# Two-block steps in the last stage, epsilon added by VectorE, and an earlier schedule of gathers and sums in the second attention

## The chip, the cores and the metric

The kernel runs on one core of one Trainium2 chip. The metric is the device time of one execution in microseconds. Engines are called PE (TensorE), DVE (VectorE), ACT (ScalarE), POOL (GpSimd) and SP (SyncE, which only issues DMAs here).

## The reference, cut to what matters

```python
x = x + tanh(g_xattn[0]) * attention_0(layernorm(x), ctx, ctx)        # 8 key groups of 8
x = x + tanh(g_ffn[0])   * experts(layernorm(x), ...)                 # 64 experts, the best 8 of each token, and a shared one
x = x + tanh(g_xattn[1]) * (attention_1(layernorm(x), ctx, ctx) @ Wc.T + bc)   # 4 key groups of 16
x = x + tanh(g_ffn[1])   * fp8_mlp(layernorm(x), w_fc, w_proj)
# fp8_mlp: both matrices and both inputs are scaled by their largest magnitude and rounded to fp8;
# h = square(relu(x8 @ w8_fc.T * scales)), rounded to fp8 again, then h8 @ w8_proj.T * scales
```

x is 64 x 64 tokens of 256 numbers, so 4096 rows: 32 tiles of 128 rows, or 8 chunks of 512.

## The kernel before, in words

x stays in SBUF. There are five stages: the first attention; the router, which scatters the rows to the experts; the experts, whose results go to DRAM (`ys`); the second attention, from about 803 to 1085 us; and the fp8 MLP. The order on each engine is written out by hand, and semaphores join the engines.

**The second attention** is a software pipeline of steps t = -3 to 35 (`second_step`, L1137). In step t an engine works on tile t and its neighbours: the normalised query of tile t+3 (`query`), the statistics of tile t+4 (`stats`, L993), the result of tile t-3 added to x (L1153), its statistics for the MLP, and the normalised tile t-4 (L1165). Into these steps the end of the experts' stage is woven for the tiles of the second half (18 tiles of 8 rows per token, 144 gathers and 144 sums):

- POOL gathers the experts' rows by indirect DMA (`gather`, L737; the instruction is L744). `asked(t)` (L733) says how many are issued before step t. Gather n first waits until gather n-5 has landed (L741), and the first of a tile waits until the tile's buffer, one of three, has been summed out.
- DVE adds each gathered row, times its weight, to x (`combine`, L1438; the instruction is L1453). `sums_within` (L1462) spreads the sums over six places of each step. The first sum of a tile waits until all 8 of its gathers have landed.
- The normalisation needs 1/sqrt(variance + epsilon). In `deviations` (L653) POOL waits for DVE's mean and variance (`mv`), adds epsilon (L663), waits for that and takes the power -0.5 (L665). In POOL's step this stands behind two of the step's gathers and ahead of the others (L720 to L729). DVE waits for the result (`rs2`, L1159) ahead of the norm and the query, for which the deviations of the step before count. The call for step t needs the statistics that DVE makes at the end of step t.

SP loads the MLP's weights and the values (V, in three parts) of the second attention while the first steps run. After some steps DVE also works on those weights: `weight_scales` (two maxima over 128x2048, L1013, after steps -1 and 0, small pieces after steps 2 and 3) and `weight_rounding` (three operations on 128x1024 after each of steps 5 to 8).

**The MLP** has a first pass (`first_pass`), which finds the largest hidden value, and a second one, the last stage of the kernel. There each of 8 chunks of 512 rows has 8 blocks f of 128 hidden features (`NF`), and each block is 128x512. For a block PE makes the product in a PSUM bank (L1879), four banks in turn. ACT takes relu with a scale (L984) into R and squares it (L978) into HS, and does the relu of the next block ahead of the square of this one. DVE rounds to a grid in three operations: CC (L1566, a bf16 result from f32), UU (L1568, bf16 from bf16 and f32) and H8 (L1572, all bf16). R, HS, CC and UU have four buffers each, used in turn. When all blocks of a chunk are rounded, PE does the 32 matmuls of the second product (`project`, L1894), which stand on PE behind the next chunk's hidden blocks. DVE ends each chunk with two operations of the chunk before (L1582, `finish`), and SP stores them. For the last chunk PE follows block by block (L1928 on), and two rows of products come after the last block.

Of the kernel before, what the change touches and what calls it, by code (L numbers as in the profile page):

```python
# [4 lines left out]
ALU = mybir.AluOpType  # L5
# [4 lines left out]
BF16 = mybir.dt.bfloat16  # L10
# [44 lines left out]
FGRP = 4  # L55
LAST = (NT + 1, NT + 3)
# [111 lines left out]
def inside(t):  # L168

    return not known(t) or 0 <= t < NT  # L170
# [37 lines left out]
def flamingo_block(nc, x_in, ctx, ctxT, gates, consts, wpairs, wsmall, wshdown, wc_in, bc_in, wfc_in, wproj_in, out):  # L208
# [128 lines left out]
    R, HS = ([carve([CH]) for _ in range(4)] for _ in range(2))  # L337
    CC, UU = ([carve([CH], BF16) for _ in range(4)] for _ in range(2))
# [134 lines left out]
    with nc.Block() as block:  # L473
# [23 lines left out]

        @block.sync
# [140 lines left out]
        def _(pool):  # L639
# [13 lines left out]
            def deviations(t, j):  # L653

                n = t + 5
                if inside(t + 4):
                    pool.wait_ge(LNA["mv"], STAT_BASE[2] + t + 5)
                if inside(t - 3):
                    pool.wait_ge(LND["mv"], t - 2)
                a, z = (j if inside(t + 4) else 3 - j), (3 - j if inside(t - 3) else j)  # L660
                at = slice(min(a, z), max(a, z) + 1, abs(z - a) or 1)
                k = 1 + (a != z)
# [132 lines left out]
        def _(act):  # L795
# [175 lines left out]
            def squares(c, j):  # L971

                def square(f):
                    n = c * NF + f
                    act.wait_ge(F["r_ready"], n + 1)
                    if past(c, 1) or f >= 4:
                        act.wait_ge(F["hu_done"], n - 3)
                    act.activation(HS[f % 4], R[f % 4], ACT.Square).then_inc(F["hs_ready"], 1)  # L978

                for f in range(NF):  # L980
                    if past(c, 1) or f >= 4:
                        act.wait_ge(F["hs_ready"], c * NF + f - 3)
                    act.wait_ge(F["h_ready"], NCH * NF // FGRP + c * NF + f + 1)
                    act.activation(R[f % 4], bank[f % 4][:, :], ACT.Relu, scale=FS[:, 22:23]).then_inc(F["r_ready"], 1)  # L984
                    if f:
                        square(f - 1)
                square(NF - 1)
# [4 lines left out]
        def _(dve):  # L992
# [62 lines left out]
            def attention(layer, a):  # L1055
# [83 lines left out]
                def second_step(t, q):  # L1139
# [34 lines left out]
                    if inside(t + 4):  # L1174
                        if t + 4 >= HT:
                            dve.wait_ge(M["cb"], ADDS * (t + 5))
                        stats(t + 4, j, ln)

                if layer == 0:
                    sweep(dve, first_step, LAST[layer], 12)  # L1180
                else:
                    stats(0, 0, ln)
                    for t in range(-3, LAST[layer] + 1):
# [378 lines left out]
            def rounding(c, j):  # L1562
                for f in range(NF):
# [4 lines left out]
                    dve.tensor_tensor(UU[f % 4], CC[f % 4], HS[f % 4], ALU.subtract).then_inc(F["hu_done"], 1)  # L1568
# [3 lines left out]
                    dve.tensor_tensor(H8[j][:, f, :], CC[f % 4], UU[f % 4], ALU.subtract).then_inc(F["h8_ready"], 1)  # L1572
# [17 lines left out]
        def _(pe):  # L1590
# [306 lines left out]
            def project(c, j):  # L1897
                pe.wait_ge(F["h8_ready"], (c + 1) * NF)
# [8 lines left out]
            def second_pass(c, j):  # L1907
                for f in range(NF):
# [5 lines left out]
                    if past(c, 1) or f >= 4:  # L1914
                        pe.wait_ge(F["r_ready"], c * NF + f - 3)
# [11 lines left out]
            for f in range(NF):  # L1927
                pe.wait_ge(F["h8_ready"], c * NF + f + 1)  # L1928
                for i in (0, 2):
                    product(j, i, f)  # L1930
# [48 lines left out]
```

## Time and profile before

| | us |
|---|---|
| median of 3 runs | 1263.76 (1261.61 to 1265.2) |
| the profiled execution | 1256.04 |
| its span | 1254.2 |
| DVE busy | 1049.4 (84%) |
| PE busy | 888.8 (71%) |
| POOL busy | 726.9 (58%) |
| ACT busy | 703.2 (56%) |
| mean granted clock of TensorE | 0.872 |

Times of the trace are microseconds from the start of the span. Shares of the whole span say little, as the stages have different limits. "Idle before" in a row is the time that the engine stood still ahead of the instruction, and the arrow names what ended it.

### The profile page before, as it was taken

The numbers are of one execution on the slowest core, as the hardware profiler recorded it, in microseconds if no ns is written. First come the engines' busy times: TensorE is split into PE (matmuls) and PEld (weight loads), VectorE is DVE, ScalarE is ACT, GpSimd is POOL, SyncE is SP. The second block draws the span as 40 slices with busy tenths as digits, with TensorE's granted clock in tenths as the row PEclk, the third lists the DMA queues.
The fourth block names the chain that finished last, engine by engine and source line by source line (L and its number), as shares of the span: only waits on it lengthen the run. The fifth ranks groups of instructions, "written<-read, shape, count | busy, mean of one in ns | idle before, by whom it ended". The sixth has DMA issues, their size and how long they took to land. (4 is left out here: it accounts for less than half of the span.)

```text
span 1254.2 us, 31305 instructions
## 1 busy us (share of the span) xinstructions
PE 888.8 (71%) x9384; PEld 630.4 (50%) x9394; DVE 1049.4 (84%) x2645; ACT 703.2 (56%) x1370; POOL 726.9 (58%) x800
## 2 busy tenths in 40 slices
PE   4789994455517787778687878657787678576665
PEld 2445552343306676767576776535555456322332
DVE  5789997988817899887699999858987778598998
ACT  3679994455406665665455666435454455426763
POOL 3467773777777777755356655267887872290000
PEclk9899995555559999999899999878899999799887
DMA  4987772222248999999799999683233330000111
GB/s 123 261 241 217 223 231 74 90 94 99 100 142 286 353 345 345 344 316 286 250 304 315 315 323 322 202 174 89 77 93 92 91 93 18 1 0 1 34 50 50
DMA packets 198115, 221.50 MB, mean 177 GB/s; under 512 B 44958, under 2 KB 176863, under 8 KB 197727
## 3 DMA queue, kind: packets, MB, share of 16 engines
q1 hardware_dynamic: 173406, 152.72, 39.4%
q0 software_dynamic: 24576, 67.14, 16.6%
q8 instruction: 68, 1.11, 0.4%
q14 instruction: 65, 0.52, 0.1%
HBM read 114.66 MB, written 105.12 MB: 175 GB/s over the span
## 5 line engine op out<-in xcount | busy, mean ns | idle before, releaser
L1745 PE MATMUL bank<-arena,region 128*128 128x128 f16 x2496 | 227.1, 229 | 2.2 <-DVE arena L1471 1.8
L767 POOL DMA_INDIRECT xs<-V x176 | 177.4, 1008 | 66.3 <-issue 50.1
L1819 PE MATMUL bank<-arena 128*128 128x128 f16 x1536 | 151.8, 223 | 69.3 <-DMA arena<-xs 68.7
L1745 PEld LDWEIGHTS bank<-arena,region 128*128 (+1 forms) x2496 | 173.3, 103 | 9.2 <-issue 2.8
L1819 PEld LDWEIGHTS bank<-arena 128*128 128x128 f16 x1536 | 102.1, 100 | 79.2 <-DMA arena<-xs 78.7
L929 ACT COPY arena<-bank 128x1024 f16<-128x1024 f16 x96 | 96.8, 1009 | 70.0 <-PE bank L1819 68.0
L814 ACT ACTIVATE arena<-bank 128x512 f32<-128x512 f32 x192 | 108.1, 605 | 46.0 <-PE bank L1629 45.5
L944 ACT CAST arena<-arena 64x512 f16<-64x512 f32 x96 | 59.3, 618 | 132.2 <-DVE arena L1487 132.2
L1076 DVE TENSOR_REDUCE arena<-bank 128x8 f32<-128x512 f32 x192 | 122.6, 679 | 12.1 <-PE bank L1615 10.4
L1848 PE MATMUL bank<-region,arena 128*128 x384 | 92.1, 279 | 47.2 <-DVE arena L1501 30.5
L744 POOL DMA_INDIRECT arena<-ys,idx x88 | 90.3, 1027 | 54.8 <-DVE x L1453 27.8
L744 POOL DMA_INDIRECT region<-ys,idx x96 | 96.0, 1000 | 27.1 <-issue 26.8
L1471 DVE COPY arena<-bank 128x1024 f16<-128x1024 f16 x96 | 65.5, 683 | 53.4 <-PE bank L1819 51.3
L1643 PE MATMUL bank<-arena 128*32 128x256 f32 (+1 forms) x768 | 74.8, 406 | 43.1 <-DVE arena L1088 43.1
L744 POOL DMA_INDIRECT V<-ys,idx x72 | 75.2, 1044 | 43.5 <-DVE x L1453 23.3
L1879 PE MATMUL bank<-region 128*128 (+1 forms) x246 | 69.9, 412 | 35.9 <-ACT arena L984 20.8
L767 POOL DMA_INDIRECT xs<-arena,V x80 | 80.1, 1001 | 24.4 <-issue 22.6
L1849 PE MATMUL bank<-region,arena 128*128 x384 | 91.5, 277 | 0.0
L1629 PE MATMUL bank<-arena,KDS 32*128 32x256 f32 (+1 forms) x768 | 79.5, 428 | 0.7 <-ACT arena L836 0.4
L1494 DVE COPY arena<-bank 128x512 f32<-128x512 f32 x96 | 66.4, 692 | 7.3 <-PE bank L1849 4.3
L1848 PEld LDWEIGHTS bank<-region,arena 128*128 128x128 f16 x384 | 37.8, 99 | 68.2 <-issue 63.3
L1487 DVE TENSOR_TENSOR arena<-bank,arena 64x512 f32<-64x512 f32 x96 | 66.6, 693 | 4.8 <-ACT arena L940 1.4
(232 smaller groups left out, 2269.9 us busy)
## 6 DMA issues: line engine op xcount, KB each, us to landing
arena<-xs SPq DMA_DIRECT2D x384, 128.0 KB
ys<-arena SPq DMA_DIRECT2D x96, 512.0 KB
xs<-idx SPq DMA_DIRECT2D x52, 256.0 KB, 3.1
arena<-in_wpairs SPq DMA_DIRECT2D x32, 256.0 KB, 2.9
arena<-in_wpairs SPq DMA_DIRECT2D x64, 128.0 KB, 3.2
out<-arena SPq DMA_DIRECT2D x16, 256.0 KB, 2.2
xs<-idx SPq DMA_DIRECT2D x8, 384.0 KB, 3.6
xs<-V POOLq DMA_INDIRECT x176
```

The lines of the kernel that those rows point to most:

```text
L744: pool.indirect_dma_start(SLOTS[half_of(t)][t % NSLOT][:, k * H:(k + 1) * H], None, ys[half_of(t)], bass.IndirectOffsetOnAxis(ap=idx[:, t, ...
L767: pool.indirect_dma_start(xs[half_of(t)], bass.IndirectOffsetOnAxis(ap=at_row[:, t, n % 8:n % 8 + 1], axis=0), ROW[t % NROW], None).then_i ...
L814: act.activation(EX[4 * j + n], bank[4 + n], ACT.Exp, scale=d ** -0.5).then_inc(a["ex_ready"], 1)
L929: act.copy(XTP[g % 2][:, 0:2], tpm[0]).then_inc(R_["xt"], 1)
L1076: dve.tensor_reduce(XG[q][:, gp * 2 * gpu:(gp + 1) * 2 * gpu, :].rearrange("p g (m w) -> p g m w", w=rp)[:, :, r * n:(r + 1) * n, 2 * d:2 ...
L1629: mm = pe.matmul(bank[4 + n][:, b * 256:(b + 1) * 256], KD[q][rows, b, :], Q2[q % 2][rows, :, b * S:(b + 1) * S], start=True, stop=True)
L1643: mm = pe.matmul(bank[1][n * cg:(n + 1) * cg, b * 256:(b + 1) * 256], VD[j][:, b, n * cg:(n + 1) * cg], EX[4 * j + n][:, b * 256:(b + 1) * ...
L1745: mm = pe.matmul(o, lhs(a, w, k), rhs(a, w, k), start=(n == 0), stop=(n == 3 * KT - 1))
L1819: mm = pe.transpose(tpm[q // 2][:, q % 2, m, :], RAW[g % 2][:, q, m * P:(m + 1) * P], rcv("ident"))
L1848: pe.matmul(o, IH[j][:, q, :], wx, start=True, stop=False)
L1849: mm = pe.matmul(o, IL[j][:, q, :], wx, start=False, stop=True)
L1879: mm = pe.matmul(bank[at][:, :], WF8[:, k, f * P:(f + 1) * P], X8[:, k, bass.ds(c * CH, CH)], start=(k == 0), stop=(k == KT - 1))
```

## The change

In the last stage the unit of work is a pair of blocks. R, HS, CC and UU have two buffers of 128x1024 in place of four of 128x512, and ACT and DVE issue 32 of each operation in place of 64. PE still makes blocks, but waits once per pair. In the second attention DVE adds epsilon itself, at the end of each step (`widened`), and POOL's `deviations` keeps the wait and the power. `asked` issues 4, 6 and 8 gathers in steps -3, -2 and -1, where 2, 2 and 3 stood, and then 4.97 per step where 5.48 stood. `sums_within` begins in step -1 where it began in step 1, does 4.97 sums per step where 5.33 stood, and ends in step 27 as it did.

```diff
+NFP = NF // 2
-    R, HS = ([carve([CH]) for _ in range(4)] for _ in range(2))
-    CC, UU = ([carve([CH], BF16) for _ in range(4)] for _ in range(2))
+    R, HS = ([carve([2 * CH]) for _ in range(2)] for _ in range(2))
+    CC, UU = ([carve([2 * CH], BF16) for _ in range(2)] for _ in range(2))
...
             def deviations(t, j):
-                if inside(t + 4):
-                    pool.wait_ge(LNA["mv"], STAT_BASE[2] + t + 5)
-                if inside(t - 3):
-                    pool.wait_ge(LND["mv"], t - 2)
-                pool.tensor_tensor(ve[:, at, :], mv[:, at, 1:2], epsilon[:, :].unsqueeze(1).to_broadcast([P, k, 1]), ALU.add).then_inc(ve2, 1)
-                pool.wait_ge(ve2, n)
+                at, k = columns_of(t, j)
+                pool.wait_ge(ve2, t + 5)
                 pool.tensor_tensor(rs[:, at, :], ve[:, at, :], neghalf[:, :].unsqueeze(1).to_broadcast([P, k, 1]), ALU.pow).then_inc(rs2, 1)
...
             def asked(t):
-                return max(2 * (t + 3), 0) if t < 0 else min(7 + (8 * HALF[1] - 7) * t // 25, 8 * HALF[1])
+                return (0, 4, 10)[t + 3] if t < 0 else min(9 + ADDS * HALF[1] * (t + 2) // 29, ADDS * HALF[1])
...
                 def square(f):
-                    n = c * NF + f
+                    n = c * NFP + f
                     act.wait_ge(F["r_ready"], n + 1)
-                    if past(c, 1) or f >= 4:
-                        act.wait_ge(F["hu_done"], n - 3)
-                    act.activation(HS[f % 4], R[f % 4], ACT.Square).then_inc(F["hs_ready"], 1)
+                    if past(c, 1) or f >= 2:
+                        act.wait_ge(F["hu_done"], n - 1)
+                    act.activation(HS[f % 2], R[f % 2], ACT.Square).then_inc(F["hs_ready"], 1)
...
+                for f in range(NFP):
+                    if past(c, 1) or f >= 2:
+                        act.wait_ge(F["hs_ready"], c * NFP + f - 1)
+                    act.wait_ge(F["h_ready"], NCH * NF // FGRP + c * NF + 2 * f + 2)
+                    act.activation(R[f % 2], bank8[:, f % 2 * 2 * CH:(f % 2 + 1) * 2 * CH], ACT.Relu, scale=FS[:, 22:23]).then_inc(F["r_ready"], 1)
...
+            def widened(t, j):
+                if inside(t + 4):
+                    dve.wait_ge(LNA["mv"], STAT_BASE[2] + t + 5)
+                if inside(t - 3):
+                    dve.wait_ge(LND["mv"], t - 2)
+                at, k = columns_of(t, j)
+                dve.tensor_scalar(ve[:, at, :], mv[:, at, 1:2], EPS, None, ALU.add).then_inc(ve2, 1)
...
                         stats(t + 4, j, ln)
+                    if inside(t + 4) or inside(t - 3):
+                        widened(t, j)
...
-                first, last = (min(max((SUM_PARTS * (t - 1) + part + z) * HALF[1] * ADDS // (SUM_PARTS * 27), 0), HALF[1] * ADDS) for z in range(2))
+                first, last = (min(max((SUM_PARTS * (t + 1) + part + z) * HALF[1] * ADDS // (SUM_PARTS * 29), 0), HALF[1] * ADDS) for z in range(2))
...
             def rounding(c, j):
-                for f in range(NF):
-                    n = c * NF + f
+                for f in range(NFP):
+                    n = c * NFP + f
                     dve.wait_ge(F["hs_ready"], n + 1)
-                    dve.tensor_scalar(CC[f % 4], HS[f % 4], SHORT_GRID, SHORT_FLOOR, ALU.mult, ALU.max).then_inc(F["hc_done"], 1)
+                    if past(c, 1) or f >= 2:
+                        dve.wait_ge(F["h8_ready"], n - 1)
+                    dve.tensor_scalar(CC[f % 2], HS[f % 2], SHORT_GRID, SHORT_FLOOR, ALU.mult, ALU.max).then_inc(F["hc_done"], 1)
...
-                    dve.tensor_tensor(H8[j][:, f, :], CC[f % 4], UU[f % 4], ALU.subtract).then_inc(F["h8_ready"], 1)
+                    dve.tensor_tensor(H8[j][:, 2 * f:2 * f + 2, :].rearrange("p f t -> p (f t)"), CC[f % 2], UU[f % 2], ALU.subtract).then_inc(F["h8_ready"], 1)
...
-                    if past(c, 1) or f >= 4:
-                        pe.wait_ge(F["r_ready"], c * NF + f - 3)
+                    if f % 2 == 0 and (past(c, 1) or f >= 4):
+                        pe.wait_ge(F["r_ready"], c * NFP + f // 2 - 1)
```

## Rows read from the trace of the kernel before

**Rows 1.** Windows: length; busy (count) PE, PEld, DVE, ACT, POOL; clock, DMA share, GB/s.
```profile
909.90:1032.50 122.60, 93.13 (x808) 63.95 (x806) 99.22 (x281) 61.09 (x138) 97.88 (x114) 0.94 0.33 93
...
1150.00:1200.00 50.00, 34.56 (x184) 19.12 (x188) 47.75 (x97) 35.74 (x61) 0.00 (x0) 0.90 0.10 32
```

**Rows 2.** Timeline, POOL: start, length, what [idle before]; between the last two, five gathers.
```profile
992.22 0.20 POOL L663 TENSOR_TENSOR ve<-mv,epsilon 128x2 f32<-128x2 f32 x1
992.50 0.72 POOL L665 TENSOR_TENSOR rs<-ve,neghalf 128x2 f32<-128x2 f32 x1
...
999.63 0.29 POOL L663 TENSOR_TENSOR ve<-mv,epsilon 128x2 f32<-128x2 f32 x1
```

**Rows 3.** Timeline, DVE: from one step's norm and query to the next one's.
```profile
984.64 0.73 DVE L1010 TENSOR_SCALAR arena<-x,mv,rs 128x256 f32<-128x256 f32 x2 [0.88 <-POOL rs L665]
...
990.92 0.34 DVE L1101 TENSOR_SCALAR arena<-KDS,cst 128x256 f16<-128x256 f32 x1
993.26 0.74 DVE L1010 TENSOR_SCALAR arena<-x,mv,rs 128x256 f32<-128x256 f32 x2 [2.00 <-POOL rs L665]
```

**Rows 4.** Timeline, POOL: deviations of steps 5, 9 and 24.
```profile
869.68 1.12 POOL L663 TENSOR_TENSOR ve<-mv,epsilon 128x2 f32<-128x2 f32 x1
...
909.99 0.23 POOL L663 TENSOR_TENSOR ve<-mv,epsilon 128x2 f32<-128x2 f32 x1
...
1032.47 0.25 POOL L663 TENSOR_TENSOR ve<-mv,epsilon 128x2 f32<-128x2 f32 x1
```

**Rows 5.** Timeline, first steps: weights' maximum, gathers 7 and 15, first sums of tiles.
```profile
820.22 2.29 DVE L1013 TENSOR_REDUCE FS<-region 128x1 f32<-128x2048 f32 x1 [4.26 <-DMA region<-in_wproj]
...
826.05 0.99 POOL L744 DMA_INDIRECT region<-ys,idx  x1 [0.18 <-issue]
827.03 1.28 DVE L1076 TENSOR_REDUCE arena<-bank 128x8 f32<-128x512 f32 x2
...
832.52 1.02 DVE L1453 SCALAR_TENSOR_TENSOR x<-region,x 128x256 f32<-128x256 f32 x2 [4.21 <-DMA region<-ys,idx]
...
840.09 0.96 POOL L744 DMA_INDIRECT arena<-ys,idx  x1 [0.30 <-issue]
...
843.07 1.00 DVE L1453 SCALAR_TENSOR_TENSOR x<-arena,region,x 128x256 f32<-128x256 f32 x2 [3.58 <-DMA arena<-ys,idx]
```

**Rows 6.** DMA, 818:824 and 824:830, the gathers' queue: packets, MB, share.
```profile
q0 software_dynamic: 208, 0.57, 46.3%
...
q0 software_dynamic: 102, 0.26, 22.1%
```

**Rows 7.** Timeline, last stage: two ends of chunks and one block between.
```profile
1165.00 1.40 DVE L1582 SCALAR_TENSOR_TENSOR arena<-bank,FS,x 128x512 f32<-128x512 f32 x2
1165.23 5.33 PE L1894 MATMUL bank<-region 128*128 128x256 bf16 x32 [1.69 <-DVE region L1572]
...
1169.43 0.42 DVE L1566 TENSOR_SCALAR arena<-arena 128x512 bf16<-128x512 f32 x1
...
1169.89 0.69 DVE L1568 TENSOR_TENSOR arena<-arena 128x512 bf16<-128x512 bf16 x1
...
1170.61 0.42 DVE L1572 TENSOR_TENSOR region<-arena 128x512 bf16<-128x512 bf16 x1
...
1178.57 1.40 DVE L1582 SCALAR_TENSOR_TENSOR arena<-bank,FS,x 128x512 f32<-128x512 f32 x2
```

**Rows 8.** Timeline, start of the first pass: DVE operations on 1024 columns.
```profile
1088.62 0.69 DVE L1043 TENSOR_SCALAR arena<-arena 128x1024 f32<-128x1024 f32 x1 [1.29 <-ACT arena L961]
...
1090.67 1.22 DVE L1527 TENSOR_TENSOR region<-arena 128x1024 bf16<-128x1024 f32 x1
```

**Rows 9.** Timeline: relu before the first block; an ACT operation on 1024 columns; PE's end.
```profile
1093.62 1.13 ACT L964 ACTIVATE arena<-region,FS 128x1024 f32<-128x1024 f32 x1
...
1138.74 1.27 ACT L984 ACTIVATE arena<-bank,FS 128x512 f32<-128x512 f32 x2 [28.64 <-DVE FS L1555]
...
1246.55 4.02 PE L1894 MATMUL bank<-region 128*128 128x256 bf16 x18 [0.91 <-DVE region L1572]
```

More of the change, by code:

```diff
@@ L496, in got_all, with columns_of @@
                 eng.wait_ge(got[i], got_count(i, 8 * (tile + 1)))
+        def columns_of(t, j):
+            a, z = (j if inside(t + 4) else 3 - j), (3 - j if inside(t - 3) else j)
+            return slice(min(a, z), max(a, z) + 1, abs(z - a) or 1), 1 + (a != z)
         @block.sync
@@ L653, in deviations @@
             def deviations(t, j):
-                n = t + 5
-                if inside(t + 4):
-                    pool.wait_ge(LNA["mv"], STAT_BASE[2] + t + 5)
-                if inside(t - 3):
-                    pool.wait_ge(LND["mv"], t - 2)
-                a, z = (j if inside(t + 4) else 3 - j), (3 - j if inside(t - 3) else j)
-                at = slice(min(a, z), max(a, z) + 1, abs(z - a) or 1)
-                k = 1 + (a != z)
-                pool.tensor_tensor(ve[:, at, :], mv[:, at, 1:2], epsilon[:, :].unsqueeze(1).to_broadcast([P, k, 1]), ALU.add).then_inc(ve2, 1)
-                pool.wait_ge(ve2, n)
+                at, k = columns_of(t, j)
+                pool.wait_ge(ve2, t + 5)
                 pool.tensor_tensor(rs[:, at, :], ve[:, at, :], neghalf[:, :].unsqueeze(1).to_broadcast([P, k, 1]), ALU.pow).then_inc(rs2, 1)
@@ L973, in square @@
                 def square(f):
-                    n = c * NF + f
+                    n = c * NFP + f
                     act.wait_ge(F["r_ready"], n + 1)
-                    if past(c, 1) or f >= 4:
-                        act.wait_ge(F["hu_done"], n - 3)
-                    act.activation(HS[f % 4], R[f % 4], ACT.Square).then_inc(F["hs_ready"], 1)
-                for f in range(NF):
-                    if past(c, 1) or f >= 4:
-                        act.wait_ge(F["hs_ready"], c * NF + f - 3)
-                    act.wait_ge(F["h_ready"], NCH * NF // FGRP + c * NF + f + 1)
-                    act.activation(R[f % 4], bank[f % 4][:, :], ACT.Relu, scale=FS[:, 22:23]).then_inc(F["r_ready"], 1)
+                    if past(c, 1) or f >= 2:
[6 more added lines that the diff above has]
+                    act.activation(R[f % 2], bank8[:, f % 2 * 2 * CH:(f % 2 + 1) * 2 * CH], ACT.Relu, scale=FS[:, 22:23]).then_inc(F["r_ready"], 1)
                     if f:
                         square(f - 1)
-                square(NF - 1)
+                square(NFP - 1)
             tiles(act, NCH, squares)
@@ L1182, in attention @@
                     stats(0, 0, ln)
+                    widened(-4, 0)
                     for t in range(-3, LAST[layer] + 1):
@@ L1562, in rounding @@
             def rounding(c, j):
-                for f in range(NF):
-                    n = c * NF + f
+                for f in range(NFP):
+                    n = c * NFP + f
                     dve.wait_ge(F["hs_ready"], n + 1)
-                    dve.tensor_scalar(CC[f % 4], HS[f % 4], SHORT_GRID, SHORT_FLOOR, ALU.mult, ALU.max).then_inc(F["hc_done"], 1)
+                    if past(c, 1) or f >= 2:
+                        dve.wait_ge(F["h8_ready"], n - 1)
+                    dve.tensor_scalar(CC[f % 2], HS[f % 2], SHORT_GRID, SHORT_FLOOR, ALU.mult, ALU.max).then_inc(F["hc_done"], 1)
                     dve.wait_ge(F["hc_done"], n + 1)
-                    dve.tensor_tensor(UU[f % 4], CC[f % 4], HS[f % 4], ALU.subtract).then_inc(F["hu_done"], 1)
+                    dve.tensor_tensor(UU[f % 2], CC[f % 2], HS[f % 2], ALU.subtract).then_inc(F["hu_done"], 1)
                     if f == 0 and past(c, 2):
@@ L1897, in project @@
             def project(c, j):
-                pe.wait_ge(F["h8_ready"], (c + 1) * NF)
+                pe.wait_ge(F["h8_ready"], (c + 1) * NFP)
                 if past(c, 2):
@@ L1913, in second_pass @@
                         spread_maxima(1, 3)
-                    if past(c, 1) or f >= 4:
-                        pe.wait_ge(F["r_ready"], c * NF + f - 3)
+                    if f % 2 == 0 and (past(c, 1) or f >= 4):
+                        pe.wait_ge(F["r_ready"], c * NFP + f // 2 - 1)
                     hidden(c, f, f % 4).then_inc(F["h_ready"], 1)
@@ L1927, in _ @@
             for f in range(NF):
-                pe.wait_ge(F["h8_ready"], c * NF + f + 1)
+                pe.wait_ge(F["h8_ready"], c * NFP + f // 2 + 1)
                 for i in (0, 2):
```

## The prediction

> **What bounds the kernel now.** I read the windows first, stage by stage, and then the timelines of the two stages that the change touches. In the last stage DVE is the limit: it is busy 47.75 of 50 us while PE, ACT and POOL are not [rows 1]. In the second attention no engine is full over the long middle (POOL 97.9 and DVE 99.2 of 122.6 us [rows 1]), so the timeline must tell. There POOL runs without a break: an addition, the power, then gathers of 0.96 us with 0.30 us between them, and the next addition at once [rows 2, 5]. DVE works 6.6 us per step (from 984.64 to the end of L1101 near 991.2) and then stands 2.00 us before the norm for POOL's `rs` [rows 3]. So here POOL sets the step, and DVE is close behind. Two things differ from that. In steps 6 to 9, which carry the weights' rounding, steps take 10.1 us (869.68 to 909.99 for four [rows 4]) and DVE has little rest. And in the first steps the loads come in: DVE waits 4.26 us for a weight matrix, 4.21 us for tile 0's gathers and 3.58 us for tile 1's [rows 5]. The DMA engines are full there.
>
> **Last stage, the pairs.** A block costs DVE 0.42, 0.69 and 0.42 us, and the ends of two chunks lie 13.57 us apart, of which 1.40 us are the finish; so a block takes (13.57 - 1.40) / 8 = 1.52 us [rows 7]. On 1024 columns the first form took 0.69 us and the second 1.22 us [rows 8]; the doubling adds 0.27 and 0.53 us. The third has no row at 1024. At 0.42 us for 512 it runs as fast as the first, so I add 0.27 us (bounds: 0 and 0.53, as for the second form). A pair is then 1.52 + 0.27 + 0.53 + 0.27 = 2.59 us where two blocks took 3.04. Saved are 0.455 us x 32 pairs = **14.6 us**, or 6.3 us at the upper bound of the third form, 23 at the lower.
>
> What is given back: before DVE's first operation ACT must do relu, relu, square. Two relus and a square of blocks took some 1.9 us (1.27 for the two relus [rows 9]); an ACT operation on 1024 columns takes 1.13 us [rows 9], so three take 3.3: +1.35 us. At the end 20 matmuls in place of 18 follow the last rounding, at 4.02 / 18 = 0.22 us each [rows 9]: +0.45 us. The new wait of DVE on `h8_ready` is for its own pair before last, so nothing queues behind it.
>
> Do two pair buffers cover as much as four block buffers? A chunk is now 4 x 2.59 + 1.40 = 11.76 us. ACT needs 8 x 1.13 = 9.0 of them. PE's 32 matmuls of the second product take 5.33 us [rows 7] and start when a chunk is rounded, 1.4 us before DVE starts the next chunk; at +4.0 us PE goes on to the blocks of the chunk after. Their first pair is there at +5.0 us, ACT does its last square of the present chunk by +5.6 us, then two relus (+7.8) and the first square (+8.9). DVE wants it at +11.76: 2.9 us of slack. So the stage gives **-12.8 us** (bounds -4.5 and -21).
>
> The Trainium skill (VectorE: DVE Perf Modes, "The TRN2 errata — SBUF-src ops pay a fixed extra latency per instruction") gives 58 cycles of 0.96 GHz as VectorE's fixed part, 0.06 us per instruction. By that a pair would save 3 x 0.06 = 0.18 us, and the 32 pairs 5.8 us, which speaks against most of this gain. The rows of this case decide otherwise: 0.69 us at 1024 and 0.42 at 512 leave 0.15 us fixed.
>
> **Epsilon on DVE.** On POOL the addition costs 0.28 us per step, from its start to the power's start [rows 2]. It goes in all steps. DVE gets one more operation on two columns behind its own `mv`, for which it must wait. No row has just this; the nearest is POOL's own addition, 0.20 us [rows 2]. I take 0.3 us with the wait (bounds 0.1, and 1.12, the longest such addition in rows 4). Behind that wait on DVE stand the next step's maxima, and with them PE. In the middle DVE has 0.9 to 2.0 us of rest per step [rows 3] to hide it, in steps 6 to 9 nothing hides it: 4 x 0.3 = 1.2 us.
>
> **The middle of the attention.** From 992.22 to 999.63 a step with five gathers took 7.41 us [rows 2]. The 15 steps from step 9 to 24 took 122.5 us, 8.17 each [rows 4], with 5.48 gathers. With 4.97 gathers and no addition POOL needs 7.41 - 0.28 = 7.13 us; DVE needs 6.6 + 0.3 = 6.9. Two engines so near each other will cost each other something, so I take 7.2 (bounds 6.9 and 7.4). 15 steps: 108 us, **-14.5 us** against before (bounds -19 and -11.5). The sums' places move with the gathers: a tile's last gather is issued about six gathers ahead of its first sum.
>
> **The first steps pay for it.** Now a sum stands in step -1, before the short keys, the query and the statistics on DVE, and it waits for gathers 0 to 7. Gather 7 is issued at 826.05 before and has landed at 832.52: 6.5 us [rows 5], under the loads. After the change it follows gather 6 at once, some 821. While the gathers' queue had work it moved 0.57 MB in 6 us [rows 6], 1.4 us per gather of 0.128 MB, so tile 0 is whole at about 827.5 (bounds 826 and 832.5, the latter as before). The end of step -1 then takes four sums of 0.5 us [rows 5], keys, query, statistics and `widened`, 3.8 us: 831.3. The first weights' maximum (2.3 us with its 2048 columns [rows 5]), which was to hide under the loads, comes behind: 833.6. Step 0 has about 4 us of work before the first sum of tile 1. POOL got step -1's `rs` done at 832.3 and needs six gathers at 1.26 us and a landing of 3.0 us (840.09 to 843.07 [rows 5]): 841.6. Then 1.5 us of rest of the step and the second maximum of 2.3 us: step 1 begins at **845.4**. Before it began at 827.03 [rows 5]: 18.4 us later (bounds 14 and 23).
>
> From there the waits for tiles 0 and 1 are behind us. DVE's steps 1 to 5 hold 5.0, 5.9, 7.0, 6.9 and 6.9 us of work (6.9 less what step 1 to 3 do not have yet, plus the small weight pieces), the four heavy ones 6.9 + 3.2 = 10.1 each (operations of 0.69 and twice 1.22 us on 1024 columns [rows 8]): 72 us, so the deviations of step 9 come at 918 where they came at 909.99 [rows 4]. The middle makes that 918 + 108 = 1026 against 1032.47: -6.5. Steps 25 to 27 are DVE's before and after, 0.3 us more each: +0.6. From there on nothing is different. So the attention gives **-5.9 us** (bounds: -5.9 - 4.5 - 4.5 = -15, and -5.9 + 4.6 + 3 = +2).
>
> The Trainium skill (DMA: Bandwidth & Descriptors, "SWDGE vs HWDGE vs iDMA") says that each DMA engine goes round-robin between the queues fed by GpSimd and those fed by the hardware path. By this rule earlier gathers would take turns from the loads and not wait behind them. The queue's 46.3% of the engines while it was kept supplied [rows 6] agrees.
>
> **The sum**: -12.8 - 5.9 = -18.7 us. The profiled execution took 1256.04 us, so its like would take 1237.3. That execution was 7.7 us under the median of the runs shown (1263.76); against the median the forecast is **1245 us**.
>
> **Rivals.**
> - Early gathers starve. With its queue supplied only from 826 on the gathers moved 0.26 MB in 6 us [rows 6]. At 2.4 us per gather until the loads are through, tiles 0 and 1 cost 7 us more in the first steps. For it: these rows. Against: part of that window had no gather to move. 1252 us.
> - Two pair buffers are too few. If the first pair of a chunk waits for PE's second product, DVE stands about 1 us at each of 7 chunks: 1252 us. Against it: 2.9 us of slack.
> - The clock, and slower than before. The last stage has 0.90 and the middle 0.94 of the clock [rows 1], with much waiting on PE in both. If the gaps now fall so that TensorE is granted 1.2 GHz most of the time, PE sets both stages. The second product takes 32 x 0.22 = 7.1 us [rows 9] and the 16 matmuls of 512 columns 16 x 0.44 = 7.1: 14.2 us per chunk, from which point (over 11.76) it decides: 8 x 2.4 = +20 us. The attention's middle would stay at 8.17 us a step: +14.5. 1245 + 34 = 1279 us. Against it: PE has the same work in less time, so it rests less.
> - It does not do what it says. The pairs save little, as at the upper bound of the third form (-6.3 + 1.8 = -4.5 us), and the gathers done early cost in the first steps all that they save later: 1259 us. For it: the first steps pay 18 us. Against it: 0.69 us at 1024 columns [rows 8].
> - The Trainium skill's figure in VectorE: DVE Perf Modes, weighed above, would lead to nearly the same place for the pairs, -5.8 + 1.8 = -4.0 us; it shares that rival's chance.
>
> **How the numbers follow.** About 0.3% (3.8 us) is what a measurement of this kernel can tell from no change. Chances: the forecast 0.62, with its own range 1236 to 1254; starving gathers 0.12; too few buffers 0.10; no effect 0.10; the clock 0.06. Slower is the clock alone, 0.06. Same is most of no effect, 0.08. Faster is the rest, 0.86. The low end, 1235, is the forecast with both stages' favourable half of their bounds (-5 and -5); the high end, 1258, takes in both rivals at 1252 with some more on either term, and leaves out the clock and no effect.
>
> **What the profile would show.** Right: DVE's three operations at 1024 columns with 0.69, 1.22 and 0.69 us and chunk ends 11.8 us apart without idle time on DVE; no addition on POOL, and its deviations 7.2 us apart in the middle; DVE waiting for a gather in step -1 until 827 or so, and step 1 beginning near 845; the deviations of step 24 near 1026. Wrong: DVE idle at chunk starts; the third operation over 0.8 us; first sums much later than 832; a granted clock well below 0.87 in the last stage; steps of 8 us in the middle, set by DVE or PE.

## The result, and the profile after the change

The changed kernel takes 1250.23 us (median of 4 runs, 1249.63 to 1252.48) where the kernel before took 1264.48 beside it (4 runs, 1261.61 to 1265.53). The ratio is 0.9893, with a 95% interval of 0.9869 to 0.9918. So it is 14.3 us faster; forecast were 18.7 us, and 1245 us as the time. 1250.23 lies in the range, 1235 to 1258. Medians here and below are of all executions of a kernel; the ratios leave out the few that lie over 1.5% above its fastest.

The profiled execution took 1250.16 us with a span of 1248.0 us. That is 5.9 us less than the one of before, but the second attention's first statistics come 5.8 us later in it (813.27 against 807.5), though nothing ahead of them was changed. Executions differ there: in the traces of the groups below that ran at ordinary speed these statistics come between 807.8 and 828.3 us. So both traces are read from these statistics on: from there to the end it was 446.8 us, and is 434.7 now.

| from the trace, us | before | after | difference | forecast |
|---|---|---|---|---|
| first statistics to the attention's end (DVE's reduction of `AM`) | 277.7 | 275.9 | -1.8 | -5.9 |
| the MLP's first pass (to the reduction of `HM`) | 51.1 | 54.2 | +3.1 | 0 |
| last stage (to the end) | 117.9 | 104.6 | -13.3 | -12.8 |

The last stage is as forecast, the attention gave a third of what was forecast, and the first pass, whose code is the same, took 3.1 us more in this execution (the changed kernel's three profiles have 54.2, 54.2 and 51.1 us; why stands in the last section).

**Last stage.** The timeline of DVE, with one chunk's end and the pair before it (start, length, and in brackets the idle time before and what ended it):

```profile
1167.28 0.68 DVE L1576 TENSOR_SCALAR arena<-arena 128x1024 bf16<-128x1024 f32 x1
1168.00 1.23 DVE L1578 TENSOR_TENSOR arena<-arena 128x1024 bf16<-128x1024 bf16 x1
1169.26 0.69 DVE L1582 TENSOR_TENSOR region<-arena 128x1024 bf16<-128x1024 bf16 x1
1169.87 1.40 DVE L1592 SCALAR_TENSOR_TENSOR arena<-bank,FS,x 128x512 f32<-128x512 f32 x2
...
1228.57 1.40 DVE L1592 SCALAR_TENSOR_TENSOR arena<-bank,FS,x 128x512 f32<-128x512 f32 x2
...
1240.31 1.40 DVE L1592 SCALAR_TENSOR_TENSOR arena<-bank,FS,x 128x512 f32<-128x512 f32 x2
```

The three operations take 0.68, 1.23 and 0.69 us, where a block took 0.42, 0.69 and 0.42 [rows 7], and chunk ends lie 11.74 us apart instead of 13.57. All that DVE waits for from 1145 us on, by its waits (engine, line, what it waited for: us in total, times, longest):

```profile
DVE arena L1576 <- ACT arena L975: 2.8, 1, 2.8
DVE arena L1592 <- DMA out<-arena: 1.8, 1, 1.8
DVE FS L1557 <- PE bank L1606: 0.6, 1, 0.6
```

The first row is the start, once; the second is the store at the very end, which stood there before too. Between them DVE never waits for ACT or PE: two pair buffers are enough.

**The middle of the attention.** Windows of steps 10 to 24 and of the last stage (length; busy and count of PE, PEld, DVE, ACT, POOL; clock, DMA share, GB/s), to be held against [rows 1]:

```profile
929.30:1036.30 107.00, 89.63 (x815) 62.39 (x813) 99.18 (x290) 61.54 (x139) 85.68 (x91) 0.98 0.34 96
1170.00:1220.00 50.00, 37.89 (x215) 22.63 (x220) 48.58 (x60) 34.74 (x34) 0.00 (x0) 0.86 0.15 51
```

15 steps take 107.0 us, 7.13 each, where they took 122.5. DVE is now busy 99 of 107 us, but POOL still sets the pace. Its busy time of 86 us leaves out some 0.3 us ahead of each gather, in which it waits for nothing that the profile shows (timeline of POOL; between the second row and the third, three more gathers):

```profile
1001.08 0.73 POOL L662 TENSOR_TENSOR rs<-ve,neghalf 128x2 f32<-128x2 f32 x1
1001.99 1.01 POOL L741 DMA_INDIRECT region<-ys,idx  x1 [0.18 <-issue]
...
1007.09 0.96 POOL L741 DMA_INDIRECT region<-ys,idx  x1 [0.30 <-issue]
1008.08 0.73 POOL L662 TENSOR_TENSOR rs<-ve,neghalf 128x2 f32<-128x2 f32 x1
```

With these pauses the 15 powers take 12.1 us and the 75 gathers 94.9, together the 107.0. DVE needs 6.75 us for a step that nothing holds up (its maxima at 984.61 and 991.36 in the trace), and is stopped twice by a gather that has not landed. DVE's waits over these steps, before and then after:

```profile
DVE arena L1010 <- POOL rs L665: 14.7, 12, 2.1
...
DVE x L1461 <- DMA arena<-ys,idx: 1.2, 1, 1.2
DVE x L1461 <- DMA region<-ys,idx: 0.9, 1, 0.9
```

DVE's new operation is short (timeline of DVE, end of one step):

```profile
990.50 0.42 DVE L992 BATCH_NORM_STATS2 st<-x 128x6 f32<-128x256 f32 x1
991.07 0.18 DVE L995 BATCH_NORM_AGGREGATE mv<-st 128x2 f32<-128x6 f32 x1
991.28 0.17 DVE L1009 TENSOR_SCALAR ve<-mv 128x2 f32<-128x2 f32 x1
991.36 1.28 DVE L1081 TENSOR_REDUCE arena<-bank 128x8 f32<-128x512 f32 x2
```

L995 ends at 991.25 and the next maxima begin at 991.36, 0.11 us behind it. Before, they began 0.08 us ahead of its recorded end (median of 15 steps). So L1009 with its wait holds DVE up by 0.2 us a step, where 0.3 were assumed.

**The first steps.** Timeline of DVE:

```profile
832.41 1.00 DVE L1461 SCALAR_TENSOR_TENSOR x<-region,x 128x256 f32<-128x256 f32 x2 [13.00 <-DMA arena<-ys,idx]
833.33 0.35 DVE L1106 TENSOR_SCALAR arena<-KDS,cst 128x256 f16<-128x256 f32 x1
...
850.32 0.48 DVE L1461 SCALAR_TENSOR_TENSOR x<-arena,region,x 128x256 f32<-128x256 f32 x1 [8.88 <-DMA region<-ys,idx]
```

DVE stands still for tile 0's gathers until 832.41 and for tile 1's until 850.32, 22 us together, and step 1 begins at 853.8. The timelines of PE and of SP's queue show what else hangs on it:

```profile
833.78 0.64 PE L1625 MATMUL bank<-arena 64*64 64x128 f16 x16 [12.87 <-issue]
834.35 2.08 PE L1639 MATMUL bank<-arena,KDS 64*128 64x256 f32 x8
...
817.40 21.71 SPq L532 DMA_DIRECT2D V<-in_ctx  x4
```

The waiting sum holds back the short keys behind it (L1106), these hold back PE's scores, and SP issues the last part of V only behind these scores (`sc_ready`): its four issues stretch over 21.7 us. In the trace of before they took 15.66 us from 811.58 on, as long after the first statistics. So tile 1's gathers now run beside V's last part. On POOL (timeline) the power of step -1 waits for DVE, and a gather for an earlier one to land:

```profile
831.48 0.94 POOL L741 DMA_INDIRECT arena<-ys,idx  x1 [1.34 <-DMA region<-ys,idx]
835.73 0.56 POOL L662 TENSOR_TENSOR rs<-ve,neghalf 128x1 f32<-128x1 f32 x1 [3.30 <-DVE ve L1009]
...
849.29 0.95 POOL L741 DMA_INDIRECT region<-ys,idx  x1 [3.42 <-DMA arena<-ys,idx]
```

Two theories for the missing 4 us came out of this. **Theory A**: it is V's last part that comes late; the sum should stand behind the keys. **Theory B**: it is the sum in step -1 itself. While DVE stands at it, POOL gets no variance and issues none of tile 1's last gathers, wherever V's part lies.

### The profile page after: what moved, and what is told of

The parts are those of the page before. It is cut to its first block and busy times, and to the rows that moved or that the text cites. A ratio compares the mean times of both kernels' runs of the same rounds, so it can differ in the third digit from the quotient of the medians.

```text
span 1248.0 us, 31031 instructions
## 1 busy us (share of the span) xinstructions
PE 884.0 (71%) x9384; PEld 632.8 (51%) x9394; DVE 1045.6 (84%) x2588; ACT 693.9 (56%) x1306; POOL 708.1 (57%) x761
## 5 line engine op out<-in xcount | busy, mean ns | idle before, releaser
L1755 PE MATMUL bank<-arena,region 128*128 128x128 f16 x2496 | 229.9, 230 | 2.3 <-DVE arena L1479 1.8
L926 ACT COPY arena<-bank 128x1024 f16<-128x1024 f16 x96 | 96.9, 1009 | 74.4 <-PE bank L1829 72.6
L811 ACT ACTIVATE arena<-bank 128x512 f32<-128x512 f32 x192 | 108.1, 604 | 40.2 <-PE bank L1639 39.9
L1653 PE MATMUL bank<-arena 128*32 128x256 f32 (+1 forms) x768 | 71.4, 396 | 33.1 <-DVE arena L1093 32.7
L1509 DVE TENSOR_TENSOR arena<-arena 64x512 f16<-64x512 f32 x96 | 66.1, 688 | 3.0
```

The lines of the kernel that those rows point to most:

```text
L811: act.activation(EX[4 * j + n], bank[4 + n], ACT.Exp, scale=d ** -0.5).then_inc(a["ex_ready"], 1)
L926: act.copy(XTP[g % 2][:, 0:2], tpm[0]).then_inc(R_["xt"], 1)
L1653: mm = pe.matmul(bank[1][n * cg:(n + 1) * cg, b * 256:(b + 1) * 256], VD[j][:, b, n * cg:(n + 1) * cg], EX[4 * j + n][:, b * 256:(b + 1) * ...
L1755: mm = pe.matmul(o, lhs(a, w, k), rhs(a, w, k), start=(n == 0), stop=(n == 3 * KT - 1))
```

## The experiments

Four kernels took one part of the change each, or moved one thing in it. In the first group of runs all kernels take some 27% longer, the kernel before too (1604.77 us, median of 25 runs). Most of that lies ahead of the second attention: its first statistics come at 1129.6 us with the pairs alone, and at 819.5 in a later trace of the same kernel, where the attention takes 304.4 and 278.1 us and the last stage 105.5 and 104.6. I call this group the slow chip, though that it was another chip is not shown: it has the number 0, and so has the last group, which ran at ordinary speed. Its traces serve for the order of events, and three of the four kernels were timed again in the later groups.

### The pairs alone

The last stage's part of the diff, with the attention of the kernel before.

> The kernel before with the pairs of the last stage alone. Theory: the last stage is a sum of DVE's own work, so it shortens by 13.4 us as it did in the changed kernel (115.6 to 102.1 us between the scale's last operation and the end), and nothing else moves; 13.4 us faster than before, ratio 0.989. The second attention stays at 277.7 us and the first pass at 53.4. Rival: part of the gain belongs to the earlier stages' new timing; then the last stage shortens by under 11 us.

1587.76 us, ratio 0.9922 (0.9884 to 0.9961). The last stage took 105.5 us. The attention did not stay at 277.7 us: it took 304.4, its middle 141.9 us with a granted clock of 0.83; what that is worth is below. At ordinary speed it was looked at again:

> The kernel before with the pairs of the last stage alone, on a chip of ordinary speed. My theory: the last stage runs 13.3 us shorter (104.6 us from its first reduction to the end in place of 117.9) and nothing else moves, so the attention still takes 278 us and the time is 13 us under the kernel before: 1250 us (1246 to 1254) where that takes 1263. Rival (the blocks' stage was set by something that the pairs do not shorten, and the gain needs the rest of the change): the last stage stays above 112 us, and the time is above 1257.

1251.63 us beside 1266.08 of the kernel before (11 runs), ratio 0.9867 (0.9822 to 0.9913): 14.5 us. The attention took 278.1 us (277.7 before), the last stage 104.6 us (117.9), and DVE's waits from 1145 us on are those of the changed kernel:

```profile
DVE arena L1569 <- ACT arena L979: 2.8, 1, 2.8
DVE arena L1585 <- DMA out<-arena: 1.8, 1, 1.8
```

The pairs do what they do in the changed kernel, alone, and are nearly its whole gain. In the same group of runs the changed kernel has a ratio of 0.9871, so the times do not tell the two apart; only the traces show what the attention's part adds.

### Epsilon on DVE alone

```diff
+                    if inside(t + 4) or inside(t - 3):
+                        widened(t, j)
...
-                pool.tensor_tensor(ve[:, at, :], mv[:, at, 1:2], epsilon[:, :].unsqueeze(1).to_broadcast([P, k, 1]), ALU.add).then_inc(ve2, 1)
-                pool.wait_ge(ve2, n)
+                pool.wait_ge(ve2, t + 5)
```

> The kernel before with epsilon on DVE alone. Theory: POOL sets the steps of the middle, so each of some 19 steps outside the weights' rounding shortens by POOL's addition, 0.28 us: deviations of steps 9 to 24 lie 118 us apart in place of 122.5, the attention takes 271 to 273 us in place of 277.7. Rival: DVE's new wait on its own mean costs the path as much as POOL saves; then 120 us or more and 276 to 279.

On the slow chip: 1627.46 us, ratio 1.0118 (1.0041 to 1.0196), slower. The middle took 152.8 us with the clock at 0.81, where the theory had 118 and its rival 120 or more. Again at ordinary speed:

> Epsilon on DVE alone once more. Theory: with the clock near full the middle (deviations of steps 9 to 24) takes 118 us in place of 122.5 and the kernel is within 0.5% of before, faster by some 5 us; with the clock down PE sets the steps and the gain is gone, or the spread of the clock hides it (the first group gave 1.0118 +- 0.008 and a middle of 152.8 us). Rival: DVE's wait lengthens PE's chain whatever the clock; then it is slower than before here too.

1255.33 us beside 1263.47 (14 runs), ratio 0.9954 (0.9915 to 0.9993). The attention took 271.2 us, 6.5 less than before, and the middle 116.1 instead of 122.6, at a clock of 0.99:

```profile
909.30:1025.40 116.10, 88.77 (x813) 62.13 (x811) 102.75 (x298) 61.22 (x138) 92.61 (x98) 0.99 0.34 96
```

From the power of step 9 to that of step 24 it is 116.2 us, and 122.5 before. So epsilon's place alone takes 0.42 us off a step. The forecast had 0.28 us for it [rows 2]. From the rows of POOL in both traces: the addition was 0.29 us with the pause ahead of it, the power no longer waits for it, 0.06, and the gathers are 0.01 us shorter each, 0.07 for a step.

### The schedule alone

`asked` and `sums_within` as in the change, everything else as before.

> The kernel before with the new schedule of gathers and sums alone, addition on POOL. Theory: step 1 begins 21 us later counted from the attention's first statistics (40 us in place of 19.6), the middle (steps 9 to 24) takes 15 x 7.4 = 111 us in place of 122.5, so the attention as a whole takes 279 to 283 us, 1 to 5 us longer than before. Rival: the schedule itself brings the attention's small gain (1.8 us in the changed kernel); then 276 us or less.

On the slow chip 1596.61 us, ratio 0.9939 (0.9896 to 0.9983). Step 1 began 40.4 us after the first statistics, as expected; the middle took 119.6 us, and 111 were expected. At ordinary speed:

> The new schedule alone once more (addition on POOL, blocks in the last stage). Theory: 0.5% or less from before: the first steps cost 21 us, the middle gives 11 to 12 where the clock is near full and up to 22 where the old schedule's longer steps lower the clock (119.6 us against 141.9 in the first group). Rival: without the addition on DVE the schedule is worth nothing in either case.

1266.19 us (10 runs) beside 1263.47, ratio 1.0000 (0.9965 to 1.0035). The attention took 282.0 us, 4.3 more than before, with the waits of the changed kernel in the first steps (timeline of DVE):

```profile
836.98 1.01 DVE L1453 SCALAR_TENSOR_TENSOR x<-region,x 128x256 f32<-128x256 f32 x2 [13.74 <-DMA region<-ys,idx]
...
854.80 0.48 DVE L1453 SCALAR_TENSOR_TENSOR x<-arena,region,x 128x256 f32<-128x256 f32 x1 [9.00 <-DMA region<-ys,idx]
```

Its middle is 9.7 us shorter (112.8), less than the 11 to 12 expected, and step 1 begins 21.4 us later: the loss is the larger.

### The sums of step -1 behind the short keys (Theory A)

```diff
+                if t == -1:
+                    first, last = (0, 4) if part == 4 else (0, 0)
```

> The changed kernel, with the four sums of step -1 moved behind that step's short keys and query. Theory: in the changed kernel the sum that waits for tile 0 holds back the short keys, so PE's first scores, and SP loads the third part of V only behind those (some 20 us later than before); tile 1's gathers then run beside that load and DVE waits 8.9 us for them. With the sums behind the keys that load starts within 8 us of the attention's start, tile 0's wait gets some us longer in its end, tile 1's shrinks to 4 us or less, and step 1 begins 3 to 6 us earlier than in the changed kernel (40.5 us from the first statistics). Rival: the load costs the gathers the same wherever it lies; the two waits keep their sum of 21.9 us and nothing is gained.

1604.32 us on the slow chip, ratio 0.9986 (0.9949 to 1.0023): nothing won. V's last part now goes through early (15.46 us for its issues), but step 1 begins 41.3 us after the first statistics (1127.9), as late as with the schedule alone on the same chip (40.4). The timeline of DVE with the first sums of tiles 0 and 1, and between them the row of POOL:

```profile
1152.45 2.05 DVE L1461 SCALAR_TENSOR_TENSOR x<-region,x 128x256 f32<-128x256 f32 x4 [14.43 <-DMA arena<-ys,idx]
...
1155.44 0.56 POOL L662 TENSOR_TENSOR rs<-ve,neghalf 128x1 f32<-128x1 f32 x1 [8.05 <-DVE ve L1009]
...
1165.79 0.48 DVE L1461 SCALAR_TENSOR_TENSOR x<-arena,region,x 128x256 f32<-128x256 f32 x1 [4.63 <-issue]
```

With V's part early, tile 0 comes 24.5 us after the first statistics (19.8 with the schedule alone), and what tile 1 wins (a wait of 4.63 us instead of 8.49) is less than the 4.7 us that tile 0 lost. POOL stands 8 us for the variance of step -1, and only then issues six gathers, the last at 1162.85, for which tile 1 waits. Theory A falls: with V's part early and the sum still in step -1, nothing is won. That V's part takes the DMA engines from whichever tile is under way fits both traces, but is argued. This kernel was not timed at ordinary speed. Theory B is left.

### No sum in step -1 (Theory B)

The changed kernel three times: as it is, with its first sums in step 0, and with its sums at the places of the kernel before (from step 1 on).

```diff
-                first, last = (min(max((SUM_PARTS * (t + 1) + part + z) * HALF[1] * ADDS // (SUM_PARTS * 29), 0), HALF[1] * ADDS) for z in range(2))
+                first, last = (min(max((SUM_PARTS * t + part + z) * HALF[1] * ADDS // (SUM_PARTS * 28), 0), HALF[1] * ADDS) for z in range(2))
```

> The changed kernel unaltered, beside the others of this group on one chip. Theory: the attention takes 276 us where the kernel before took 277.7, in the first steps 21 us more and in the middle 15 us less; on a chip where the middle's steps are set by PE at a lower granted clock (0.82 to 0.83 in the middle of the two kernels of the first group that kept the old schedule) the whole gain is near 1%, as measured. If the lower clock hits the denser schedule as well, the middle comes to over 125 us.

> The changed kernel with the sums beginning in step 0 in place of step -1 (5.14 per step, end in step 27 as before). Theory, formed on the run with the sums behind the keys (its load of V came early, tile 1's wait was gone, and still step 1 began at 41.3 us, since POOL stood 8 us for epsilon of step -1, which DVE makes behind the sum that waits): what costs is that a sum stands in step -1 at all, so that POOL's next eight gathers wait for DVE, and DVE for POOL's. With no sum there POOL goes on, and step 1 begins at 30 to 34 us from the first statistics; the attention is 6 to 9 us shorter than the changed kernel's at the same middle. Rival: the gathers under the loads are limited by the DMA engines and not by POOL's waiting; then step 1 begins at 37 or later and the gain is under 3 us.

> The changed kernel with the sums at the places of the kernel before (none before step 1), the gathers as in the change. My theory: the 8 us that the first steps lose come from the sums of step -1 and 0, which wait for gathers under the loads, and POOL's next gathers in turn wait for step -1's epsilon. Without them tile 1 is waited for less and step 1 begins 18 to 24 us after the first statistics (40.5 with the change); the 15 middle steps have 6% more sums each and take 108 to 112 us (107); the attention takes 266 to 270 us (275.9), and the time is 1239 to 1244 us where the changed kernel takes 1247. Rival (the early sums are work that has to be done anyway, and waiting for the loads only shows there): what the first steps win comes back in the middle as longer steps, of 7.6 us and more; the attention takes 274 us or more and the time is that of the change, 1247.

> The changed kernel with the first sums in step 0 in place of step -1, timed once more beside the changed kernel. My theory, from its first profile: step 1 begins 30 us after the first statistics (40.5 with the change), the attention takes 268 us (275.9), so the time is 6 to 8 us under the changed kernel: 1239 to 1242 us where that takes 1247. Rival (the stages behind give it back, as the first timing with 1243.7 against 1246.3 could mean): 2 to 3 us under the changed kernel.

> The changed kernel beside the others of this group, as their yardstick. Theory: 1246 to 1250 us, 1% under the kernel before, with the attention of 275 to 276 us and the last stage of 104.6 as in its first two profiles. Rival: the attention's first steps depend on how the loads happen to fall, and then the attention's length differs by more than 3 us from these.

| | median, us | ratio to before (95%) | step 1 begins | attention |
|---|---|---|---|---|
| changed kernel | 1246.34 | 0.9843 (0.9805 to 0.9881) | 40.7 | 275.0 |
| the same, next group | 1249.44 | 0.9871 (0.9829 to 0.9913) | 39.3 | 274.0 |
| sums from step 0 | 1243.74 | 0.9822 (0.9775 to 0.9868) | 30.0 | 268.2 |
| the same, next group | 1244.27 | 0.9815 (0.9770 to 0.9859) | 30.0 | 268.2 |
| sums from step 1, same group | 1242.76 | 0.9814 (0.9772 to 0.9856) | 22.8 | 269.1 |

("Step 1 begins" and "attention" are counted from the first statistics.) Both variants take 5 to 8 us off the attention of the changed kernel, and step 1 begins at 30.0, inside what was expected of the first of them. By the medians it is 2.6 and 5.2 us for sums from step 0 and 6.7 us for sums from step 1; by the ratios 2.7, 7.1 and 7.2. The 2.6 holds one execution of 1257.48 us among four, whose first statistics come only at 828.3 us; without it the median is 6.4 us under the changed kernel's. The 5.2 of the second group misses the 6 to 8 us that were expected; the ratio's 7.1 does not. The intervals of each ratio still overlap with the changed kernel's, so the times alone do not prove the gain; the attention's length, the same to 0.1 us in both profiles of sums from step 0, is the firmer witness. These two are the fastest kernels of this study.

What this shows of theory B has a limit. Without a sum in step -1 both delays go: POOL's power of that step comes 18.8 us after the first statistics (22.5 with the change), and V's last part goes through early too (15.3 us for its issues). The run before showed that V's part alone is not enough; whether the sum could go and V's part stay late was not tried.

The kernel with sums from step 1 was expected to have a middle of 108 to 112 us and has 107.9 (window):

```profile
844.80:930.50 85.70, 56.48 (x456) 38.05 (x454) 70.16 (x180) 36.51 (x78) 63.76 (x63) 0.82 0.36 93
930.50:1038.40 107.90, 86.72 (x807) 60.79 (x807) 101.10 (x297) 61.29 (x138) 85.21 (x92) 1.00 0.34 96
```

What it wins at step 1 (17.7 us against the changed kernel's first profile) it gives back in part up to step 9: 85.7 us where that takes 75.5. There it waits for POOL. DVE's waits from the first statistics to step 9 (822 to 931 us); of the 20.4 us in the first row, 12.4 lie behind the beginning of step 1:

```profile
DVE arena L1015 <- POOL rs L662: 20.4, 9, 7.2
DVE arena L1502 <- PE bank L1859: 1.7, 1, 1.7
DVE FS L1018 <- DMA region<-in_wproj: 0.8, 1, 0.8
```

No wait for a gather is left. POOL's gathers stand ahead of its power, and wait for landings themselves, so DVE now waits for the gathers at second hand. So the rival of its expectation came true in part: of the 17.7 us, 10.2 are given back before step 9 and 0.9 in the middle.

With the sums at their old places this kernel's attention takes 269.1 us, and 268.2 with sums from step 0, where epsilon alone took 271.2. So the new schedule of gathers is worth some 2 to 3 us, hardly more than the changed kernel's own profiles differ (274.0 to 275.9), and most of what the attention gained in any kernel here is epsilon's.

## Why the prediction was right, and where it was off

The parts add up. Against 277.7 us of attention, epsilon alone gives -6.5 and the schedule alone +4.3, together -2.2; the change's profiles have -1.8, -2.7 and -3.7. The last stage gives -13.3 in the first two of them and -12.8 in the third.

- **The pairs** (forecast -12.8): right in its main terms. A pair takes 2.59 us, as forecast; chunk ends 11.74 (11.76). The start cost 2.77 us of waiting against 1.5 before, +1.3 (forecast +1.35). The end did not cost 0.45 us: 20 matmuls took 3.89 us where 18 took 4.02 [rows 9]. The third form, which had no row at 1024 columns, took 0.69 us as assumed. The rival with the fixed part of 0.06 us (taken there from the Trainium skill, VectorE: DVE Perf Modes) is out: the pairs' 32 x 2.60 us (means of 684, 1225 and 691 ns) against the blocks' 64 x 1.54 save 15 us. That was half a reading of the page: the same section of the Trainium skill goes on to say that the measured fixed term is about 150 cycles, and 0.15 us is what the rows of this case give too.
- **The middle** (forecast 108 us): 107.0. The mechanism was right: POOL still sets the step, at the 7.13 us that the forecast had worked out for it, with nothing lost to DVE being near (it had added 0.07 for that). The split is nearly additive: epsilon alone -6.4, the schedule alone -9.7, both -15.5.
- **Tile 0** (forecast at 827.5, 20 us after the first statistics): it came at 832.41, 19.1 after them. Right.
- **Tile 1** (forecast 34.1 after the first statistics): 37.1. Here the step "POOL got step -1's `rs` done and needs six gathers and a landing of 3.0 us" failed: the gathers issued up to 843.1 had landed only before 850.3, some 7 us. V's last part ran beside them (from 839 to 850 us the loads' queue took 81% of the DMA engines' time); with V's part early, in the run with the sums behind the keys, the last gather of tile 1 was issued at 1162.85 and DVE went on at 1165.79, 2.9 us later. Step 1 began 40.5 us after the first statistics instead of 37.95: 2.5 us.
- **Steps 1 to 9** (forecast 72): 75.5. Counted to POOL's powers, the four heavy steps took 38.9 (forecast 40.4) and steps 1 to 5 took 36.6 instead of 31.7; counted to DVE's own addition it is 40.2 and 35.1. DVE's work in steps 1 to 5 was counted rightly (30.84 us busy), but it waits there for what POOL issues (its waits from 853.8 to 890.4; the 2.5 us end at 885.63, at the first sum of tile 3, whose last gather POOL issued at 881.87):

```profile
DVE x L1461 <- issue: 2.5, 1, 2.5
DVE x L1461 <- DMA region<-ys,idx: 1.1, 2, 0.7
DVE arena L1015 <- POOL rs L662: 0.5, 1, 0.5
```

  POOL runs seven gathers in step 1 and five in each of the others without a break (timeline):

```profile
861.38 0.58 POOL L662 TENSOR_TENSOR rs<-ve,neghalf 128x1 f32<-128x1 f32 x1
...
868.86 0.63 POOL L662 TENSOR_TENSOR rs<-ve,neghalf 128x1 f32<-128x1 f32 x1
...
875.85 0.73 POOL L662 TENSOR_TENSOR rs<-ve,neghalf 128x2 f32<-128x2 f32 x1
```

  The power of step 1 comes 7.6 us after that step's beginning, and the one of step 2 another 7.5 us later, where the forecast gave these steps DVE's 5.0 and 5.9 us. So the term that failed is the first steps as DVE's work alone: the sum that the forecast had made for POOL in the middle (7.13 us) was left out here.
- **The attention in all**: +2.5 us at step 1, +2.9 up to the deviations of step 9 (75.5 against the 918 - 845.4 = 72.6 of the forecast) and -1.0 in the middle: 4.4 us short of the forecast, and by its ends 4.1. With that, and 0.5 us more from the last stage, the sum would have been -18.7 + 4.1 - 0.5 = -15.1; the medians gave -14.3. The attention's forecast of -5.9 us was three times the -1.8 measured, and the time fell into the range because the pairs carry most of the gain.
- **The rivals.** Starving gathers: the price named for it (7 us in the first steps) is near the 5.4 us found up to step 9, and the cause is a kin of it, though the gathers were held up by V's last part and by POOL's own waits more than by the loads of the weights. Its 1252 us is closer to the measured time than the forecast. Two buffers too few: DVE's waits exclude it. The clock: 0.86 in the last stage and 0.98 in the middle; it fell a little in the first and rose in the second, and set neither at ordinary speed.

What the prediction did not weigh is what else hangs on DVE's new wait. In step -1 it does not only cost DVE's own time: POOL, PE and SP each wait for something that DVE does behind it. The text named the keys, query and statistics there, and priced them as DVE's 3.8 us alone.

## What to carry to other kernels

Moving work earlier in a hand-written order pays only if its inputs are there: ask of the engine that would wait what stands behind the wait and which other queues are fed from it. Here the early gathers brought 2 to 3 us at most and the early sums cost 5 to 8 us of the attention. And where two engines both run nearly full, the one with the longer sum sets the step, so each step has to be summed for both, the first ones too, with the pauses that an engine's busy time leaves out.

## What the runs showed of the hardware

**The shared port.** The first pass takes 49.9, 51.1 or 54.2 us with the same instructions. The 7 operations of line 1531 before (1539 after) take 1012 ns on average in the trace of before, 1384 in that of after and 786 with sums from step 1. In the timeline of before, DVE and POOL:

```profile
1097.86 2.76 DVE L1531 TENSOR_SCALAR arena<-arena 128x1024 f32<-128x1024 f32 x1
...
1097.70 2.37 POOL L786 TENSOR_TENSOR arena<-arena 128x1024 f32<-128x1024 f32 x1
```

and with sums from step 1:

```profile
1103.57 0.68 DVE L1539 TENSOR_SCALAR arena<-arena 128x1024 f32<-128x1024 f32 x1
...
1103.62 2.84 POOL L783 TENSOR_TENSOR arena<-arena 128x1024 f32<-128x1024 f32 x1
```

Whichever starts first runs at its own pace, and the other takes longer by nearly what the first still has to run: DVE 2.76 us instead of 0.7 behind POOL's, POOL 2.84 instead of 2.37 behind DVE's. POOL started 0.16 us ahead of DVE in the one and 0.05 us behind it in the other, and that decides over 2 us. The Trainium skill (SBUF — State Buffer, "SBUF: two separate sides") says that VectorE and GpSimd share a pair of ports which whichever starts first holds for its whole instruction; the trace agrees. In these traces it is worth 4 us per execution. No edit is needed to shift it: the changed kernel's third profile has 1012 ns and a first pass of 51.1 us, as the kernel before had.

**The clock on the slow chip.** There the granted clock in the attention's middle was 0.83 with the pairs alone, 0.81 with epsilon alone, 0.93 with the schedule alone and 0.87 with the sums behind the keys, and the 15 steps took 141.9, 152.8, 119.6 and 134.5 us. The window of epsilon alone:

```profile
1249.00:1401.80 152.80, 103.78 (x794) 71.12 (x793) 100.25 (x291) 58.59 (x135) 90.88 (x97) 0.81 0.27 74
```

DVE's work is the same 100 us there, and it stands 29.5 us ahead of the maxima (L1080) and 17.9 us ahead of the normalisation (L1088), both of which read what PE has put into its banks (the profile names PE as what ended 9.8 us of this, and no engine for the rest). PE's matmuls of line 1708 (256 columns) took 495 ns on average, and 388 with the same kernel at ordinary speed. The same epsilon edit thus measures 1.0118 in one group of runs and 0.9954 in another. This is what the clock's rival described: with a low clock PE sets the step. There is one profile per kernel here, and none of the kernel before. Why the clock is lower there stays open, and so does whether sparse work lowers the clock or the low clock makes the work sparse.
